# Two 256-column chunks of a short job as one step: one PSUM bank, one cast, one subtraction

## What is computed

```python
xn = _layernorm(x)
# branch 1: an exponential moving average along the tokens (as an FFT convolution), then SiLU
attn = silu(irfft(rfft(xn) * rfft(k)) + xn * omega)
# branch 2: R = 4 rounds of a mixture of E = 4 experts, two experts for each token
for r in range(R):
    logits = flat @ Wg[r] + bg[r]
    vals, idx = top_k(logits, 2);  w = softmax(vals)         # cw: weights, zero for experts not chosen
    hmid = gelu(einsum('nh,ehf->enf', flat, W1) + b1)        # H = 128 -> F = 512
    y = einsum('enf,efh->enh', hmid, W2) + b2
    cur = cur + einsum('ne,enh->nh', cw, y)
out = x + attn + cur
```

## Time and profile before

| | us |
|---|---|
| median of three runs | 632.57 |
| span of the profiled execution, first to last instruction | 631.1 |
| PE busy | 596.3 (94%) |
| DVE busy | 472.9 (75%) |
| ACT busy | 511.1 (81%) |
| POOL busy | 391.3 (62%) |
| granted TensorE clock, mean | 0.988 of full |

### The profile page before, as it was taken

How to read it: one execution, slowest core, us unless ns; L and a number is a source line. 1 busy time by engine, 2 the same in 40 slices (tenths; PEclk the granted TensorE clock), 3 DMA queues, 4 the chain that set the end, 5 groups by cost and what they waited for, 6 DMA issues and landing times.

```text
span 631.1 us, 11206 instructions
## 1 busy us (share of the span) xinstructions
PE 596.3 (94%) x3317; PEld 497.1 (79%) x3317; DVE 472.9 (75%) x1079; ACT 511.1 (81%) x982; POOL 391.3 (62%) x393
## 2 busy tenths in 40 slices
PE   8899999999999999999999999999999999999991
PEld 7678887877878888788878888788878888878880
DVE  6997956689976998559975798559965788677681
ACT  4889788888888879778888889778888889878880
POOL 6656478352883468643884468643884368688765
PEclk9989999999999999999999999999999999999996
DMA  8311034665966689667976789567976789799951
GB/s 235 101 37 34 2 95 136 213 226 216 336 251 222 258 299 361 210 229 257 333 257 224 266 280 375 198 221 283 319 253 227 267 277 377 211 269 299 375 169 37
DMA packets 64746, 145.67 MB, mean 231 GB/s; under 512 B 8567, under 2 KB 33838, under 8 KB 60206
## 3 DMA queue, kind: packets, MB, share of 16 engines
q1 hardware_dynamic: 56788, 134.12, 60.1%
q0 software_dynamic: 7424, 10.56, 6.3%
q10 hardware_dynamic: 474, 0.28, 0.2%
HBM read 36.11 MB, written 12.09 MB: 76 GB/s over the span
## 4 chain that ended last, share of the span: by engine, by line
PE 56%; POOL 20%; DVE 11%; issue 7%; ACT 3%; POOLq 1%; DMA 1%; DVEq 0%; SPq 0%; ACTq 0%
POOL sorted_rows L841 10%; PE y L1546 9%; PE z L1526 8%; PE y L1547 8%; PE y L1548 8%; PE z L1529 7%; PE z L1532 7%; POOL state L827 5%; PE spare L1448 5%; DVE h_lo L1345 3%; POOL out_dram L862 3%; PE misc L1470 2%; PE misc L1469 2%; DVE weighted L1266 1%; DMA rows<-in_L_ffn_W_dram 1%
## 5 line engine op out<-in xcount | busy, mean ns | idle before, releaser
L1345 DVE TENSOR_TENSOR h_lo<-z,h_hi 128x512 fp32r<-128x512 f32 (+1 forms) x432 | 250.9, 592 | 79.3 <-ACT h_hi L997 76.6
L994 ACT ACTIVATE z<-z,w_job 128x512 f32<-128x512 f32 (+1 forms) x368 | 213.4, 580 | 59.2 <-PE z L1532 53.7
L997 ACT CAST h_hi<-z 128x512 fp32r<-128x512 f32 (+1 forms) x432 | 221.8, 513 | 13.7
L827 POOL TENSOR_TENSOR state<-state,weighted 128x512 f32<-128x512 f32 (+1 forms) x90 | 107.0, 1188 | 100.3 <-DVE weighted L1266 99.2
L841 POOL DMA_INDIRECT sorted_rows<-rows,position_i x112 | 120.1, 1073 | 36.4 <-issue 19.6
L1526 PE MATMUL z<-cur_hi,w_job 128*128 128x512 f32 (+2 forms) x368 | 136.8, 372 | 0.1
L1546 PE MATMUL y<-h_hi,w_job 128*128 128x512 f32 (+1 forms) x368 | 131.7, 358 | 5.2 <-DVE h_lo L1345 4.8
L1529 PE MATMUL z<-cur_lo,w_job 128*128 128x512 f32 (+2 forms) x368 | 128.4, 349 | 0.0
L1532 PE MATMUL z<-cur_hi,w_job 128*128 128x512 f32 (+2 forms) x368 | 128.2, 349 | 0.0
L1547 PE MATMUL y<-h_lo,w_job 128*128 128x512 f32 (+1 forms) x368 | 128.2, 348 | 0.0
L1548 PE MATMUL y<-h_hi,w_job 128*128 128x512 f32 (+1 forms) x368 | 128.1, 348 | 0.0
(11 more groups left out here) (164 smaller groups left out, 775.6 us busy)
## 6 DMA issues: line engine op xcount, KB each, us to landing
w_job<-w_all SPq DMA_DIRECT2D x35, 1026.5 KB, 5.4
w_job<-w_all SPq DMA_DIRECT2D x57, 514.5 KB, 5.6
w_job<-w_all SPq DMA_DIRECT2D x57, 512.0 KB, 5.6
gate_bc<-gate_rows SPq DMA_DIRECT2D x71, 256.0 KB, 4.0
rows<-sorted_rows SPq DMA_DIRECT2D x28, 266.0 KB, 4.5
gate_bc<-gate_rows SPq DMA_DIRECT2D x37, 128.0 KB, 3.1
x_tok<-in_L_attn_x_dram SPq DMA_DIRECT2D x8, 256.0 KB, 5.5
out_dram<-x_tok SPq DMA_DIRECT2D x8, 256.0 KB, 5.7
```

Source lines behind the costliest of these rows:

```text
L827: pool.tensor_tensor(state[job.g][:, cols_at], before, weighted[:, j % TR, 0:job.n], ALU.add).then_inc(added, 1)
L994: nc.scalar.activation(zs, zs, ACT.Gelu_apprx_tanh, bias=bias).then_inc(gelu_done, 1)
L997: nc.scalar.copy(h_hi[:, s % ZR, 0:job.n], zs).then_inc(hi_act, 1)
L1345: dve.tensor_tensor(h_lo[:, s % ZR, 0:job.n], zs, hs.bitcast(F32), ALU.subtract).then_inc(lo_done, 1)
```

## The change

Steps become units. A unit holds one chunk of a full job, a half or a dense job, and two chunks of a short one (X). The two z chunks lie side by side in one PSUM bank, columns 0 to 255 and 256 to 511. ACT waits for both, applies Gelu twice (the bias differs by chunk) and casts once over 512 columns; DVE subtracts once over 512 columns. PE does six matmuls for `up` and six for `down` of such a unit. LAG, ZR and all else stay. A sorted phase has 42 units in place of 52 steps, the last 46 in place of 56. All tables are written in units. `combine(j)` comes one unit after the first unit of the next job, `unit_end(j) + 1`, and the add one later.

```diff
+def unit_list():
+    units, first = [], []
+    for j, job in enumerate(JOBS):
+        first.append(len(units))
+        together = 2 if job.kind == "X" else 1
+        units += [Unit(j, range(c, c + together)) for c in range(0, FC, together)]
+    return units, first
...
 def combine_at(j):
     late = DENSE_PHASE["combine"]
-    return late[j] if j < len(late) else FC * (j + 1) + 1
+    return late[j] if j < len(late) else unit_end(j) + 1
...
 SORTED = {
-    "P": (42, 44, 51, 53), "P copy": (46, 48, 53, 57), "P split": (44, 46, 49, 55),
-    "P logits": (46, 51, 54, 57), "I": (46, 52, 55, 59), "I copy": (49, 55, 59, 62),
-    "I split": (47, 56, 59, 63), "G": 49, "G copy": 52, "ema": (22, 25, 27, 30, 34, 36), "ema tanh": 36,
-    "A": 39, "A add": 41, "gates": (7, 8, 8, 10), "tanh": 13, "weights": 15, "count": 16, "ranks": 15,
-    "places": (17, 18), "pairs": (22, 22), "order": 21, "pick": 27, "jobs": 31, "table": 35,
-    "scatter": (19, 20, 20, 20, 21, 23, 24, 24, 25, 27, 31, 33, 35, 35, 40, 42), "ema 2": (2, 3, 4, 5, 6, 9),
+    "P": (32, 34, 41, 43), "P copy": (36, 38, 43, 47), "P split": (34, 36, 39, 45),
+    "P logits": (36, 41, 44, 47), "I": (36, 42, 45, 49), "I copy": (39, 45, 49, 52),
+    "I split": (37, 46, 49, 53), "G": 39, "G copy": 42, "ema": (19, 20, 21, 24, 27, 28), "ema tanh": 28,
+    "A": 29, "A add": 31, "gates": (7, 8, 8, 10), "tanh": 13, "weights": 15, "count": 16, "ranks": 15,
+    "places": (17, 17), "pairs": (19, 19), "order": 19, "pick": 21, "jobs": 25, "table": 27,
+    "scatter": (17, 18, 18, 18, 18, 19, 20, 20, 20, 21, 25, 26, 27, 27, 30, 32), "ema 2": (2, 3, 4, 5, 6, 9),
...
 LAST_PHASE = {
-    "P": (38, 41, 47), "P add": (41, 44, 50), "finish": (42, 45, 51), "idents": 1,
-    "gather": (8, 10, 25, 27, 29, 30, 31, 32, 33, 34, 35, 36), "Q": (54, 55), "Q add": (57, 58),
+    "P": (28, 31, 37), "P add": (31, 34, 40), "finish": (32, 35, 41), "idents": 1,
+    "gather": (8, 10, 20, 21, 22, 23, 23, 24, 24, 25, 25, 26), "Q": (44, 45), "Q add": (47, 48),
...
         @block.scalar
...
-                    act.wait_ge(z_full, s + 1)
-                    nc.scalar.activation(zs, zs, ACT.Gelu_apprx_tanh, bias=bias).then_inc(gelu_done, 1)
-                    if not hi_on_dve(s):
-                        act.wait_ge(gelu_done, s + 1)
-                        nc.scalar.copy(h_hi[:, s % ZR, 0:job.n], zs).then_inc(hi_act, 1)
+                    act.wait_ge(z_full, FC * j + chunks[-1] + 1)
+                    for c in chunks:
+                        zc = z[:, s % ZR, chunk_cols(s, c)]
+                        bias = b_all[:, job.e, c:c + 1] if job.kind == "D" else b_job[:, slot(job), c:c + 1]
+                        nc.scalar.activation(zc, zc, ACT.Gelu_apprx_tanh, bias=bias).then_inc(gelu_done, 1)
+                    act.wait_ge(gelu_done, FC * j + chunks[-1] + 1)
+                    nc.scalar.copy(h_hi[:, s % ZR, 0:width(s)], z[:, s % ZR, 0:width(s)]).then_inc(hi_act, 1)
...
         @block.vector
...
-                    dve.wait_ge(hi_act, hi_count(s, False))
-                dve.tensor_tensor(h_lo[:, s % ZR, 0:job.n], zs, hs.bitcast(F32), ALU.subtract).then_inc(lo_done, 1)
+                dve.wait_ge(hi_act, s + 1)
+                dve.tensor_tensor(h_lo[:, s % ZR, 0:width(s)], z[:, s % ZR, 0:width(s)],
+                                  h_hi[:, s % ZR, 0:width(s)].bitcast(F32), ALU.subtract).then_inc(lo_done, 1)
...
         @block.tensor
...
             def up(s):
...
+                for c in chunks:
+                    hi, lo = w1(job, c)
+                    dst = z[:, s % ZR, chunk_cols(s, c)]
+                    pe.matmul(dst, hi, cur_hi[job.g][:, here], start=True, stop=False)
...
             def down(s):
...
                 pe.wait_ge(lo_done, s + 1)
...
+                for c in chunks:
+                    hi, lo = w2(job, c)
```

More of the change, by code:

```diff
@@ L82, with unit_end, width @@
 NJ = len(JOBS)
-STEPS = FC * NJ
+Unit = namedtuple("Unit", "j chunks")
+def unit_list():
[5 more added lines that the diff above has]
+    return units, first
+UNITS, FIRST_UNIT = unit_list()
+STEPS = len(UNITS)
+def unit_end(j):
+    return FIRST_UNIT[j + 1] if j + 1 < NJ else STEPS
+def width(s):
+    return len(UNITS[s].chunks) * JOBS[UNITS[s].j].n
 def combine_at(j):
     late = DENSE_PHASE["combine"]
-    return late[j] if j < len(late) else FC * (j + 1) + 1
+    return late[j] if j < len(late) else unit_end(j) + 1
 def block_done(p, b):
@@ L142 @@
 LAST_PHASE = {
-    "P": (38, 41, 47), "P add": (41, 44, 50), "finish": (42, 45, 51), "idents": 1,
-    "gather": (8, 10, 25, 27, 29, 30, 31, 32, 33, 34, 35, 36), "Q": (54, 55), "Q add": (57, 58),
-    "Q finish": (57, 58)}
+    "P": (28, 31, 37), "P add": (31, 34, 40), "finish": (32, 35, 41), "idents": 1,
+    "gather": (8, 10, 20, 21, 22, 23, 23, 24, 24, 25, 25, 26), "Q": (44, 45), "Q add": (47, 48),
+    "Q finish": (47, 48)}
 BEFORE_LAST = {
-    "P add": (43, 46, 53, 55), "stores": (46, 47, 48, 49, 51, 54, 57, 58, 64, 65, 66, 68, 70, 72, 73, 75), "idents": 22}
+    "P add": (33, 36, 43, 45), "stores": (36, 37, 38, 39, 41, 44, 47, 48, 54, 55, 56, 58, 59, 60, 60, 61), "idents": 19}
 EMA_PHASE = (1, 1, 2, 2, 3, 4, 5, 6)
@@ L438, in ema_and_routed_ffn_kernel @@
         hi_act = sem("hi_act")
-        hi_dve = sem("hi_dve")
         lo_done = sem("lo_done")
@@ L509, in parts_in, with chunk_cols @@
             return job_w2_in[n], 16 * sum(slot(job) == n and job.kind in ("F", "H") for job in JOBS[DENSE:j + 1])
-        def hi_count(s, on_dve):
-            return sum(hi_on_dve(n) == on_dve for n in range(s + 1))
+        def chunk_cols(s, c):
+            n = JOBS[UNITS[s].j].n
+            at = UNITS[s].chunks.index(c) * n
+            return slice(at, at + n)
         def where(name):
@@ L677, in _ @@
                 for b in range(B):
-                    if j == ADD_AT["A", b] // FC + 3:
+                    if j == UNITS[ADD_AT["A", b]].j + 3:
                         store_x(b)
@@ L876, in _ @@
             for s in range(-1, STEPS):
-                for j in range(max(s // FC - 3, 0), s // FC + 1):
+                now = UNITS[max(s, 0)].j
+                for j in range(max(now - 3, 0), now + 1):
                     if combine_at(j) + 1 == s and not add_on_dve(j):
@@ L986, in _ @@
             for s in range(STEPS):
-                    j, c = divmod(s, FC)
+                    j, chunks = UNITS[s]
                     job = JOBS[j]
-                    zs = z[:, s % ZR, 0:job.n]
-                    if c == 0 and job.kind != "D":
+                    if chunks[0] == 0 and job.kind != "D":
                         act.wait_ge(*parts_in(j))
-                    bias = b_all[:, job.e, c:c + 1] if job.kind == "D" else b_job[:, slot(job), c:c + 1]
-                    act.wait_ge(z_full, s + 1)
-                    nc.scalar.activation(zs, zs, ACT.Gelu_apprx_tanh, bias=bias).then_inc(gelu_done, 1)
-                    if not hi_on_dve(s):
-                        act.wait_ge(gelu_done, s + 1)
-                        nc.scalar.copy(h_hi[:, s % ZR, 0:job.n], zs).then_inc(hi_act, 1)
+                    act.wait_ge(z_full, FC * j + chunks[-1] + 1)
[5 more added lines that the diff above has]
+                    nc.scalar.copy(h_hi[:, s % ZR, 0:width(s)], z[:, s % ZR, 0:width(s)]).then_inc(hi_act, 1)
                     if s == 0:
@@ L1334, in _ @@
             for s in range(STEPS):
[L1335 to L1343, removed]
-                    dve.wait_ge(hi_act, hi_count(s, False))
-                dve.tensor_tensor(h_lo[:, s % ZR, 0:job.n], zs, hs.bitcast(F32), ALU.subtract).then_inc(lo_done, 1)
+                j = UNITS[s].j
+                dve.wait_ge(hi_act, s + 1)
+                dve.tensor_tensor(h_lo[:, s % ZR, 0:width(s)], z[:, s % ZR, 0:width(s)],
+                                  h_hi[:, s % ZR, 0:width(s)].bitcast(F32), ALU.subtract).then_inc(lo_done, 1)
                 for earlier in range(max(j - 3, 0), j + 1):
@@ L1506, in up @@
             def up(s):
-                j, c = divmod(s, FC)
+                j, chunks = UNITS[s]
                 job = JOBS[j]
-                if c == 0:
+                if chunks[0] == 0:
                     if j == 0:
@@ L1522, in up @@
                         pe.wait_ge(job_w1_in[slot(job)], 16 * uses(j))
-                hi, lo = w1(job, c)
                 here = bass.ds(extra_cols[job.i], HALF) if job.kind == "X" else job_cols(job)
[L1525 to L1532, removed]
+                for c in chunks:
+                    hi, lo = w1(job, c)
+                    dst = z[:, s % ZR, chunk_cols(s, c)]
+                    pe.matmul(dst, hi, cur_hi[job.g][:, here], start=True, stop=False)
+                    if s == 0:
+                        pe.wait_ge(cur_ready, 1)
+                    pe.matmul(dst, hi, cur_lo[job.g][:, here], start=False, stop=False)
+                    if s == 0:
+                        pe.wait_ge(w_lo, 1)
```

(14 more changed lines are left out.)

4 lines of the change are left out of this document (1 added, 3 removed).

## The result

The changed kernel takes 649.11 us (median of four runs, 647.74 to 649.55) against 632.71 us of the kernel before beside it: ratio 1.0247, 95% interval 1.0232 to 1.0263. It is slower by 16 us. The forecast was 651.7 us in a range of 640 to 657. That the time lies in it is in part luck: as the experiments show, its 8.4 us for falls of the clock behind P0 did not come, and costs that it did not count took their place.

The account below looks back on a forecast made before the run. POOL's queue, from the row positions to X4's add, was taken to set P0. 632.57 + 13.05 (later P0) - 2.3 (last phase) gave 643.3, plus 8.4 for clock falls 651.7 us; range 640 to 657.

Parts of the forecast that it names:

- What bounds the kernel: Phases 1 to 5: PE until the next F3, then DVE's positions, then POOL's scatters and adds, which P0 waits for.
- The positions come later: Sort in phases 1 to 6: three more `up` delay F3's end by 1.05 us, so positions come 0.8 us later.
- POOL's order: POOL's queue ahead of P0: F3's add falls behind the first scatter, into the busy queue, costing 1.4 us per phase.
- The total of both steps: P0 in phases 1 to 5: 0.8 us for later positions plus 1.4 for POOL's queue, 2.2 us later.
- The lead of PE: Short jobs: running three units ahead, PE waits 1.2 us less per phase for h_lo and the job table.
- The clock: Behind P0, phases 1 to 6: longer PE idle time drops the clock, 1.4 us per fall, 8.4 us in all.
- The last phase: Phase without a scatter of positions: PE's waits for h_lo go, and the end comes 2.3 us earlier.
- The sum: Phases 1 to 6: 13.05 us for later P0 plus 8.4 us for falls of the clock.
- The first term: P0 in phases 1 to 6 coming later, 5 x 2.2 + 2.05 = 13.05 us.
- The second term: One fall of the clock after each P0 of phases 1 to 6, 6 x 1.4 = 8.4 us.
- rival 1: P0 waits longer for POOL's queue but the clock stays up, 643.3 us; chance 0.30, including one to three falls.
- Rivals 2 and 3: Faster, P0 not waiting for POOL's queue, 623 us, chance 0.08; no change, costs and gains cancelling, 632.6 us, chance 0.04.

Follow-up runs that it names:

- Run 3: Kernel after with short jobs' weights loaded in two pieces, the W1 piece no longer waiting for a combine; 656.2 us against 632.7 of the kernel before.
- run 1: Kernel before with one table entry changed, the first scatter issued at step 17, ahead of F3's add on POOL; 636.2 us, ratio 1.0048.
- run 4: Kernel after with short jobs' weights loaded in two pieces and F3's add back ahead of the first scatter; 653.6 us, ratio 1.0325.
- run 6: Kernel before with the next phase's sort two steps earlier, first scatters at 16 to 20; 663.2 us against 657.0 of the kernel before, ratio 1.0103.
- run 11: Kernel before with the sort one or two steps earlier where PE doesn't wait for it; 644.1 us against 652.8 of the kernel before, ratio 0.9864.
- runs 5 and 9: Kernel after with weights in two pieces plus 28 unused transposes before PE's wait at P0, run twice; 658.0 and 654.6 us, ratios 1.0014 and 1.0029.

## Why the prediction was right, and where it was not

- **What bounds the kernel** (POOL's queue, from the positions to X4's add, sets P0): right. Run 3 isolates it: in phase 4 PE arrives 3.7 us early and P0 doesn't come a moment sooner; in phases 1 and 3, where PE had come last, it comes 0.5 us sooner.
- **The positions come later**: F3's end by 1.05 us as forecast, the positions by 0.4 and not 0.8. The step left out that F3's add, by leaving its place, frees DVE of a neighbour that had cost it 0.45 us.
- **POOL's order, +1.4 us**: in phase 4 the queue grew from 25.8 to 27.2, as forecast, but it is made up otherwise: the adds take 1.8 us more (F3's, and 0.5 on the others), the gaps 0.55, the scatters 1.0 less. And the move itself is worth 0.3 us net in both kernels (runs 1 and 4), since each shift changes what lies beside what. With the add back in its old place (run 4) P0 of phase 4 still comes 1.5 us later than in the kernel before, 1.0 of it by the later positions and 0.5 by a longer queue: most of the delay comes from the three more `up` ahead of F3's end, not from the add. The total of both steps, 2.2 us, was near: P0 of phases 4 and 5 came 1.8 us later. In phase 6 it was 3.3, not 2.05, for there the queue grew by 3.0 us (24.7 to 27.7).
- **"The lead of PE", 1.2 us less waiting**: wrong. The step counted h_lo and the job table and left out the other side of a longer lead: what `up` reads must be there earlier too. X4's `up` waits 1.8 to 2.8 us for weights in each of phases 1 to 6, and X3's and X4's 2.1 and 0.8 us in the last. The combine, moved a chunk later, was never followed to the SyncE queue that waits for it.
- **The clock, +8.4 us**: the mechanism is right, its place not. Idle time of 3.7 us ahead of P0 drops the clock every time (12 of 12 in runs 3 and 4), and each fall cost 2.0 us in run 3 where I took 1.4. But in the changed kernel P0's idle time is 0 to 1.8 us, no fall lies behind it, and the term is worth nothing. Three falls came ahead, behind the waits for X4's weights.
- **The last phase, -2.3 us**: it took 1.0 us more. The waits for h_lo among its short jobs are gone, waits for X3's and X4's weights have come. With 1.3 us of the latter left (run 3) its P0 comes 0.8 us earlier than in the kernel before, so the gain was also put too high.
- **The sum**: for phases 1 to 6 the forecast had 13.05 + 8.4 = 21.45 us, measured are 13.8, 7.6 less. The first term nearly came: P0 is 13.9 us later over the six phases, against 13.05. Run 3 has 12.6 of this by POOL's queue alone; the waits for X4's weights, their three falls of the clock included, add only about 1.3. The second term, 8.4, did not come at all.
- **Why the total was near all the same**: against the 8.4 stand the last phase, 3.3 us too low, and 1.4 us in places that I had at nothing; the 0.9 of it ahead of phase 1 is within what differs between traces (123.2 to 124.9 us on this chip). By the traces the forecast is 7.6 - 3.3 - 1.4 = 2.9 us too high, by the medians 2.6. So the nearness of 651.7 to 649.1 is luck. What came is nearest to rival 1, the queue without the clock, at 643.3: with 0.8 for P0, 3.3 and 1.4 it gives 648.8. Rivals 2 and 3 fell with the result, and run 1 shows that the queue has no slack.

What stays open: why phases of the same program differ so much with the sort moved (run 6, phases 3 and 4), what makes run 11 faster, what in the second and third chip makes the last phase 5 to 10 us longer, and whether the kernel after would be slower by 2.5% on those chips too.

## What to carry to other kernels

A coarser step is a longer lead, and a lead has two ends: results are waited for less, but whatever the leading engine reads (weights, gates, buffers freed by a later stage) is needed sooner. Follow both ends, through every queue, before counting a gain. Where an in-order queue on a slow engine sets the end, rounding a table to coarser steps can change who goes first in it. What that costs is not the length of the instruction that moved: here an add of 1.3 us cost 0.3 net, as its neighbours ran faster. And a wait that is removed in one place of a bounded loop becomes idle time in another, which is not always free: here it was cheaper for PE to wait twice for 2 us than once for 4.

## What the runs showed of the hardware

- Removing a wait of PE made the kernel slower by 7 us (run 3 against the kernel after) because the idle time, gathered in one place, dropped TensorE from 2.4 to 1.2 GHz. Keeping PE occupied with 28 transposes, 3.2 us, kept it at 2.4 GHz in 12 of 12 cases and took 10 to 11 us back in phases 1 to 6 (runs 5 and 9).
- The clock's fall is not told by the idle time alone: it fell after 1.83 us (phase 4) and not after 2.70 (phase 5), PE having been busy around both. The Trainium skill (TensorE: Matmul & The Clock Gate, on oscillation in real kernels) speaks of longer waits than that; here the shorter ones did it too.
- A small DVE instruction beside POOL's add takes several times its time: 0.71 instead of 0.25 us for 128x96 (L1194), and in the kernel after 1.13 us for 32x18, where the same took 0.16 before:

```profile
379.92 1.13 DVE L1231 TENSOR_TENSOR in_a<-starts,job_c 32x18 f32<-32x18 f32 x1
```

  POOL's add runs from 379.71 to 381.01. In the kernel before, another 128x96 instruction beside the same add, which reads one of its inputs (`misc`) from PSUM, took 0.26 us (L1189). That GpSimd shares its SBUF interfaces with VectorE, with contention for instructions of two SBUF inputs, is what the Trainium skill says (GPSIMD Engine Reference, Specifications); the traces agree.
- The same program takes 632.7, 652.8 and 657.0 us on three chips. The kernel before has a trace on the first alone; in the traces of the other kernels the last phase differs, up to P0 (51 to 53 us on the first chip, 57 to 63 on the others), and hardly behind it (33 to 35).
